# The delta scan split eleven to five: the larger part in PSUM on VectorE, the smaller on GpSimd, sums on TensorE

## The reference: what is computed

```python
Sk = jnp.einsum('bhde,bhe->bhd', Sm, k_t)
delta = v_t - Sk
Sm = Sm + beta_t[..., None] * jnp.einsum('bhd,bhe->bhde', delta, k_t)
o_t = jnp.einsum('bhde,bhe->bhd', Sm, q_t)
```

## Time and profile before

| what | value |
|---|---|
| median of 3 runs | 2863.08 us |
| span of the profiled execution | 2862.5 us |
| PE, DVE, ACT, POOL busy | 1846.5, 1859.1, 941.8, 992.1 us |
| stage 2, from 1169.70 to 1586.05 us | 416.3 us |
| in 1173.8 to 1586.0: PE, DVE, POOL busy | 247.3, 366.2, 248.4 us |

### The profile page before, as it was taken

How to read it: one execution, slowest core, us unless ns; L and a number is a source line. 1 busy time by engine, 2 the same in 40 slices (tenths; PEclk the granted TensorE clock), 3 DMA queues, 4 the chain that set the end, 5 groups by cost and what they waited for, 6 DMA issues and landing times. The chain is left out here.

```text
span 2862.5 us, 43966 instructions
## 1 busy us (share of the span) xinstructions
PE 1846.5 (65%) x9776; PEld 929.6 (32%) x9776; DVE 1859.1 (65%) x5482; ACT 941.8 (33%) x1955; POOL 992.1 (35%) x1512
## 2 busy tenths in 40 slices
PE   2499999998407913366566107447999999950493
PEld 1133333333305702233333004322333333350373
DVE  6488778784512237899999358558888888643123
ACT  2256656566102300000000003233656656720131
POOL 3022222223373410455665055301222222336442
PEclk8589999999558956676776558767999999965697
DMA  2501111110013450000000300130111111001344
GB/s 71 196 22 25 26 26 25 25 25 2 5 50 115 133 137 4 0 0 0 0 0 4 33 15 15 44 99 28 31 26 26 24 25 24 2 0 40 94 137 128
DMA packets 109051, 120.23 MB, mean 42 GB/s; under 512 B 31248, under 2 KB 71568, under 8 KB 107664
## 3 DMA queue, kind: packets, MB, share of 16 engines
q1 hardware_dynamic: 92304, 96.50, 13.1%
q0 software_dynamic: 8192, 16.86, 1.7%
q10 hardware_dynamic: 8320, 4.19, 0.6%
HBM read 71.01 MB, written 45.71 MB: 41 GB/s over the span
## 5 line engine op out<-in xcount | busy, mean ns | idle before, releaser
L719 DVE CUSTOM_DVE_ANT_0 pA<-pA,causal 128x512 f32<-128x512 f32 (+3 forms) x1536 | 823.6, 582 | 181.2 <-PE pA L562 168.5
L763 ACT ACTIVATE wt<-pB 128x512 f32<-128x512 f32 (+3 forms) x1536 | 653.9, 496 | 441.1 <-PE pB L603 435.4
L804 POOL TENSOR_SCALAR_AFFINE_SELECT wt<-wt 128x128 f32<-128x128 f32 x1024 | 290.6, 293 | 766.5 <-ACT wt L763 745.7
L562 PE MATMUL pA<-ka,qa 125*128 125x512 bf16 (+3 forms) x1536 | 487.2, 343 | 66.6 <-PEq L258 30.0
L603 PE MATMUL pB<-qa,ka 128*128 128x512 bf16 (+3 forms) x1536 | 450.5, 337 | 42.5 <-ACT wt L763 19.4
L1594 PE MATMUL g_pq<-g_proq,ident 128*128 128x256 f32 x512 | 247.3, 651 | 179.0 <-POOL g_proq L1547 179.0
L619 PE MATMUL pC<-wt,va 128*32 128x512 f32 (+3 forms) x3072 | 345.6, 497 | 0.3
L603 PEld LDWEIGHTS pB<-qa,ka 128*128 128x128 bf16 x1536 | 145.3, 97 | 418.8 <-ACT wt L763 256.0
L1594 PEld LDWEIGHTS g_pq<-g_proq,ident 128*128 128x128 f32 x512 | 138.5, 278 | 287.5 <-POOL g_proq L1547 207.2
L562 PEld LDWEIGHTS pA<-ka,qa 125*128 125x128 bf16 x1536 | 147.6, 98 | 249.5 <-DVE mx L719 163.6
L719 DVE DVE_READ_ACCUMULATOR2_ANT mx<- 128x1 f32 x1536 | 216.8, 141 | 0.0
(11 more groups left out here) (219 smaller groups left out, 2163.0 us busy)
## 6 DMA issues: line engine op xcount, KB each, us to landing
w<-in_L_ffn_fc_w_dram SPq DMA_DIRECT2D x64, 256.0 KB
qa<-qk_parts SPq DMA_DIRECT2D x192, 64.0 KB
ka<-qk_parts SPq DMA_DIRECT2D x192, 64.0 KB
xi<-xin SPq DMA_DIRECT2D x32, 258.0 KB
qk_parts<-qp SPq DMA_DIRECT2D x24, 256.0 KB, 2.4
qk_parts<-kp SPq DMA_DIRECT2D x24, 256.0 KB, 2.8
xin<-zero SPq DMA_DIRECT2D x4, 1032.0 KB, 7.1
y<-zero SPq DMA_DIRECT2D x4, 1024.0 KB, 12.6
```

The costliest lines, as they stand in the source:

```text
L562: pe.matmul(slot(s, n)[:, 0:b - a], qa[s.stage][0:MROW, h, i * P:(i + 1) * P], ka[s.stage][0:MROW, h, a:b], start=True, stop=True).then_in ...
L719: vec.tensor_tensor_reduce(out=slot(s, n)[:, 0:size], in0=slot(s, n)[:, 0:size], in1=mask, scale=1.0, scalar=LOWEST, op0=ALU.add, op1=ALU.max,
L763: act.activation(wt[g % NW][h][:, 0:e - a], pB[(g * GH + h) % NB][:, 0:e - a], ACT.Exp).then_inc(exp_done, 1)
L804: pool.affine_select(out=block_, in_=block_, compare_op=ALU.is_ge, fill=0.0, base=0, pattern=[[1, P]], channel_multiplier=-1).then_inc(mas ...
```

## The change

The heads are divided eleven to five in place of eight and eight, and each part stays with one engine. VectorE keeps eleven heads, with their matrix `Rv` in PSUM; GpSimd keeps five in `Rg` in SBUF. Each engine makes the key products, the outer products, the updates and the query products of its own heads. The sum over the last index and the subtraction of the values move to TensorE for both: eight matmuls against the identity and one against minus the identity, into `uv` (which VectorE reads in PSUM) and `pu` (which ScalarE copies to `ug` for GpSimd, which has no operand in PSUM here). The PSUM buffer of the query sums is doubled. TensorE's order for a token j is: deltas of VectorE's heads for j+1, deltas of GpSimd's heads for j+1, query sums of j. At the start the first matrix is made in SBUF and copied to PSUM by VectorE, and at the end it is copied back for the store, which is two DMAs now.

```diff
...
         FULL = [P, H, R2, HD]
...
+        HV = 11
+        HG = H - HV
+        PART_V, PART_G = [P, HV, R2, HD], [P, HG, R2, HD]
+        V_LINKS = 2
+        G_LINKS = 2
         with ExitStack() as in2:
             sb2 = lambda n, s, dt=F32: core.sb(in2, "g2_" + n, s, dt)
+            ps2 = lambda n, s, dt=F32: core.ps(in2, "g2_" + n, s, dt)
             sem2 = lambda n: core.sem(in2, "g2_" + n)
...
+            Rv, uv = ps2("Rv", PART_V), ps2("uv", [P, 512])
+            uv = uv[:, 0:HV * R2].rearrange("p (h r) -> p h r", r=R2)
+            Rg, ug = sb2("Rg", PART_G), sb2("ug", [P, HG, R2])
+            prod_v, prod_g = sb2("prod_v", PART_V), sb2("prod_g", PART_G)
             proq = [sb2(f"proq{i}", FULL) for i in range(2)]
...
+            minus = sb2("minus_ident", [P, P])
+            pu = ps2("pu", [P, HG, R2])
+            pq = [ps2(f"pq{i}", [P, H * R2]) for i in range(2)]
+            start, copied, chain_v, chain_g, kv_mult, uv_sum, kg_mult, ug_sum, ug_kept, qv_mult, qg_mult, q_sum, q_kept, end_kept, stored = (
+                sem2(n) for n in ("start", "copied", "chain_v", "chain_g", "kv_mult", "uv_sum", "kg_mult", "ug_sum", "ug_kept", "qv_mult",
+                                  "qg_mult", "q_sum", "q_kept", "end_kept", "stored"))
+
+            def heads(a, j, at, first, count):
+
+                begin = at + first * HD
+                return a[:, bass.ds(j, 1), begin:begin + count * HD].rearrange("p o (h r) -> p (o h) r", r=HD)
             def tokens(eng, one):
...
                 one(SEG - 2, 0)
                 one(SEG - 1, 1)
+            def more(j):
+                return not isinstance(j, int) or j < SEG - 1
+
+            def reused(j):
+                return not isinstance(j, int) or j >= 2
+
             with nc.Block() as block:
                 @block.gpsimd
                 def _(pool):
...
+                    pool.memset(prod_v[:, :, :, :], 0.0).then_inc(start, 1)
+                    pool.memset(Rg[:, :, :, :], 0.0).then_inc(start, 1)
+                    pool.memset(minus[:, :], 0.0).then_inc(start, 1)
+                    pool.wait_ge(start, 3)
+                    for whole, count in ((prod_v, HV), (Rg, HG)):
+                        eye = whole[:, :, HD:, :]
+                        pool.affine_select(out=eye, in_=eye, compare_op=ALU.not_equal, fill=1.0, base=0,
+                                           pattern=[[0, count], [1, HD], [-1, HD]], channel_multiplier=0).then_inc(start, 1)
+                    pool.affine_select(out=minus[:, :], in_=minus[:, :], compare_op=ALU.not_equal, fill=-1.0,
+                                       base=0, pattern=[[-1, P]], channel_multiplier=1).then_inc(start, 1)
                     def multiply(j):
...
+                        pool.tensor_tensor(prod_g[:, :, :, :], Rg[:, :, :, :],
+                                           heads(qkvb, j, D, HV, HG).unsqueeze(2).to_broadcast(PART_G),
+                                           ALU.mult).then_inc(kg_mult, 1)
                     def token(j, n):
...
+                        pool.wait_ge(ug_kept, j + 1)
+                        pool.tensor_tensor(prod_g[:, :, :, :], ug[:, :, :].unsqueeze(3).to_broadcast(PART_G),
+                                           heads(kbeta, j, 0, HV, HG).unsqueeze(2).to_broadcast(PART_G),
+                                           ALU.mult).then_inc(chain_g, 1)
+                        pool.wait_ge(chain_g, j * G_LINKS + 1)
+                        pool.tensor_tensor(Rg[:, :, :, :], Rg[:, :, :, :], prod_g[:, :, :, :],
+                                           ALU.subtract).then_inc(chain_g, 1)
+                        pool.wait_ge(chain_g, j * G_LINKS + 2)
+                        if more(j):
                             multiply(j + 1)
...
+                        if reused(j):
                             pool.wait_ge(q_sum, j - 1)
...
+                        pool.tensor_tensor(proq[n][:, HV:, :, :], Rg[:, :, :, :],
+                                           heads(qkvb, j, 0, HV, HG).unsqueeze(2).to_broadcast(PART_G),
+                                           ALU.mult).then_inc(qg_mult, 1)
+
+                    pool.wait_ge(start, 6)
                     multiply(0)
                     tokens(pool, token)
                 @block.vector
                 def _(vec):
...
+                    vec.wait_ge(start, 6)
+                    vec.tensor_copy(Rv[:, :, :, :], prod_v[:, :, :, :]).then_inc(copied, 1)
+                    vec.wait_ge(copied, 1)
                     def multiply(j):
...
+                        vec.tensor_tensor(prod_v[:, :, :, :], Rv[:, :, :, :],
+                                          heads(qkvb, j, D, 0, HV).unsqueeze(2).to_broadcast(PART_V),
+                                          ALU.mult).then_inc(kv_mult, 1)
+
+                    def query(j, n):
+                        if reused(j):
+                            vec.wait_ge(q_sum, j - 1)
+                        vec.tensor_tensor(proq[n][:, 0:HV, :, :], Rv[:, :, :, :],
+                                          heads(qkvb, j, 0, 0, HV).unsqueeze(2).to_broadcast(PART_V),
+                                          ALU.mult).then_inc(qv_mult, 1)
                     def token(j, n):
...
+                        vec.wait_ge(uv_sum, j + 1)
+                        vec.tensor_tensor(prod_v[:, :, :, :], uv.unsqueeze(3).to_broadcast(PART_V),
+                                          heads(kbeta, j, 0, 0, HV).unsqueeze(2).to_broadcast(PART_V),
+                                          ALU.mult).then_inc(chain_v, 1)
+                        vec.wait_ge(chain_v, j * V_LINKS + 1)
+                        vec.tensor_tensor(Rv[:, :, :, :], Rv[:, :, :, :], prod_v[:, :, :, :],
+                                          ALU.subtract).then_inc(chain_v, 1)
+                        vec.wait_ge(chain_v, j * V_LINKS + 2)
+                        if more(j):
                             multiply(j + 1)
+                        query(j, n)
                     multiply(0)
                     tokens(vec, token)
+                    vec.tensor_copy(prod_v[:, :, :, :], Rv[:, :, :, :]).then_inc(end_kept, 1)
                 @block.tensor
                 def _(pe):
+                    flat = lambda v: v.rearrange("p h r -> p (h r)")
+
+                    def vector_deltas(j):
+
+                        pe.wait_ge(kv_mult, j + 1)
+                        reached(pe, chain_v, j * V_LINKS)
+                        for e in range(HD):
+                            pe.matmul(flat(uv), c["ident"][:, :], flat(prod_v[:, :, :, e]), start=e == 0, stop=False)
+                        pe.matmul(uv[:, :, 0:HD], minus[:, :], heads(qkvb, j, 2 * D, 0, HV),
+                                  start=False, stop=True).then_inc(uv_sum, 1)
+
+                    def pool_deltas(j):
+
+                        pe.wait_ge(kg_mult, j + 1)
+                        reached(pe, ug_kept, j)
+                        for e in range(HD):
+                            pe.matmul(flat(pu[:, :, :]), c["ident"][:, :], flat(prod_g[:, :, :, e]),
+                                      start=e == 0, stop=False)
+                        pe.matmul(pu[:, :, 0:HD], minus[:, :], heads(qkvb, j, 2 * D, HV, HG),
+                                  start=False, stop=True).then_inc(ug_sum, 1)
+
                     def token(j, n):
...
+                        if more(j):
+                            vector_deltas(j + 1)
+                            pool_deltas(j + 1)
+                        pe.wait_ge(qv_mult, j + 1)
+                        pe.wait_ge(qg_mult, j + 1)
+                        if reused(j):
+                            pe.wait_ge(q_kept, j - 1)
                         for e in range(HD):
...
+                            last = pe.matmul(pq[n][:, :], c["ident"][:, :], flat(proq[n][:, :, :, e]),
                                              start=e == 0, stop=e == HD - 1)
                         last.then_inc(q_sum, 1)
+                    pe.wait_ge(start, 6)
+                    vector_deltas(0)
+                    pool_deltas(0)
                     tokens(pe, token)
                 @block.scalar
                 def _(act):
...
+                    def keep_delta(j):
+                        act.wait_ge(ug_sum, j + 1)
+                        act.copy(ug[:, :, :], pu[:, :, :]).then_inc(ug_kept, 1)
+
+                    def token(j, n):
+                        if more(j):
+                            keep_delta(j + 1)
                         act.wait_ge(q_sum, j + 1)
...
+                        act.copy(outs[:, bass.ds(j, 1), :, :].rearrange("p o h r -> p (o h r)"), pq[n][:, :]).then_inc(q_kept, 1)
+
+                    keep_delta(0)
+                    tokens(act, token)
                 @block.sync
                 def _(sp):
...
+                    sp.wait_ge(chain_g, SEG * G_LINKS)
+                    sp.dma_start(w["segments"][:, HV:, :].rearrange("p h x -> p (h x)"),
```

(31 more changed lines are left out.)

18 lines of the change are left out of this document (removed).

## The result

The changed kernel takes 2947.31 us, the median of 4 runs (2941.5 to 2950.78), beside 2865.79 us for the kernel before in 4 runs (the three above and one more): a ratio of 1.0286, 95% interval 1.0265 to 1.0307. It is 82 us slower; 2948 was forecast. The profiled execution has a span of 2939.8 us, 77.3 more than that of before.

A forecast was written before the change was run, and what follows sets the result against it. VectorE, with its waits for GpSimd, was taken to bound the scan at 12.56 us a token; TensorE at 15.3 us would replace it. The scan goes from 416.3 to 500.7 us, +84.4, giving 2948 us, range 2932 to 2990.

The forecast's parts named there:

- The main term: Scan: TensorE becomes the bound, 8192 strided column reads a token, 15.2 to 15.8 us, taken as 15.3.
- V: TensorE's group in the scan for the deltas of VectorE's heads: 5.3 us a token.
- P: TensorE's group in the scan for the deltas of GpSimd's heads: 2.5 us a token.
- Q: TensorE's query sums of the token before, in the scan: 7.4 us a token.
- the proportional end: TensorE's strided reads in the scan cost 1.80 ns a column and record: 14.75 us a token.
- the fixed part: Other end for TensorE's strided reads: 0.035 us a record plus 1.67 ns a column, 15.35 us a token.
- The clock: TensorE in the scan: busy throughout at clock 1.00, yet strided columns stay at 1.80 ns at either clock.
- The cover: Scan: P and Q, 9.9 us, cover VectorE's 5.0 us between V groups, even 9.8 with PSUM instructions twice as long.
- the rival in which a wait for VectorE takes TensorE's place: Scan: VectorE over 3.2 us an instruction in PSUM, loop above 15.3 us, time above 2948; 10% together with loads that show.
- The ends: Scan's start and finish: first V after 7.8 us, 18.1 until TensorE stops waiting, then to 500.7 us against 416.3 before.
- The rival that TensorE would stream at the contiguous price: Scan: strided matmuls at 0.84 ns a column, 7.6 us a token, 255 us, total 2702 us; chance 6%.
- Rival "loads stop hiding": TensorE in the scan: weight loads show behind narrow matmuls, 1.5 us a token, 48 us, 2996; 10% together with VectorE's wait.

The follow-up runs named there:

- e1: Changed kernel with matrices and all products stored last index first, so TensorE's operands are contiguous, plus a copy back at the end: 2731.59 us, ratio 0.9546.
- e3: Changed kernel with VectorE's key product made twice, once into a spare tile: 2950.4 us, ratio 1.0304 to the kernel before.
- e4: Changed kernel with the matrix of VectorE's eleven heads in SBUF in place of PSUM: 2951.01 us, ratio 1.0313 to the kernel before.
- e7: Changed kernel, query products only, with two of the eight last elements side by side (TensorE stride 8 bytes): 2833.58 us, ratio 0.9901.
- e2: Changed kernel with only the query products stored last index first, delta groups still at stride eight: 2822.66 us, ratio 0.9857.
- e5: Kernel of e1 with the matrix of VectorE's heads in SBUF in place of PSUM: 2777.68 us, ratio 0.9703 to the kernel before.

## Why the prediction was right, point by point

- The main term. 15.3 us of TensorE a token were forecast, 15.23 measured. Of its parts, V was put at 5.3 us and takes 5.30 (1401.96 to 1407.26), P at 2.5 and takes 2.51 (to 1409.77), Q at 7.4 and takes 7.42 (to 1417.19). The choice between the ends, proportional to columns or with a fixed part a record, is settled for the proportional end: 80 columns take 2.35 / 16 = 0.147 us a record (0.144 by proportion, 0.168 with the fixed part), 176 columns 5.10 / 16 = 0.319 (0.317 or 0.328). The 0.1 us that was added for waits between groups is not there: the groups join without a gap. The sum is closer than its terms: the strided columns take 14.87 us (14.75 forecast), the values 0.36 (0.45), the waits nothing (0.1).
- The clock. TensorE is at 1.00 from 1194 us on, as forecast, and the strided records didn't speed up. At the start of the scan it isn't: the first V begins at 0.50 and the second has a stretch of 0.50 in it, and they take 5.26 and 5.18 us from their start to the matmuls with the values, where V takes 5.10 at 1.00. In e1, with contiguous operands, the first takes 4.68 at 0.52 and a later one 2.48 at 0.99. So the price of the strided columns hardly depends on the clock here either.

```profile
1177.90:1180.00 2.10, 2.03 (x6) 0.50 0.00 0
```

- The cover. P and Q were said to cover VectorE's round of 5.0 us and even 9.8 us. e3 lengthened it by 1.6 us and e4 by 0.9, and the time stayed; no run made it as long as 9.8. VectorE's instructions were put at 1.60 us and take 1.61 to 1.63, far from the 3.2 us of the rival in which a wait for VectorE takes TensorE's place; GpSimd's at 1.45 and take 1.29 for the product with `kbeta` and 1.54 or 1.55 for the others, in sum 5.9 (5.8).
- The ends. The scan was put at 500.7 us and takes 499.15. The first V was to start 7.8 us after the first memset and does so 8.0 after (1177.97 - 1169.97); the wait for the second V, 5.0 less the 2.5 of P by the terms of the prediction, is 2.53. In the timeline of the start and the end:

```profile
1169.97 1.27 POOL L1539 MEMSET g_prod_v<- 128x1408 f32 x1 [152.83 <-POOLq L1351]
...
1177.97 5.44 PE L1623 MATMUL g_uv<-g_prod_v,ident 128*128 128x176 f32 x16 [18.70 <-DVE g_prod_v L1586]
...
1188.64 5.35 PE L1623 MATMUL g_uv<-g_prod_v,ident 128*128 128x176 f32 x16 [2.53 <-DVE g_prod_v L1586]
```

```profile
1669.12 0.32 SPq L1696 DMA_DIRECT2D g_Rt<-segments  x1
```

- The figure. That 2948 and 2947.31 are less than 1 us apart is luck: the scan came out 1.6 us shorter than forecast, the median of the kernel before is 2.7 us higher with its fourth run than with three, and the four runs of each of the two kernels spread over 9 and 10 us. What the runs bear out is the +84.4 us of the scan, where +82.8 was measured, and the terms that it is made of.
- The rival that TensorE would stream at the contiguous price is refuted for this kernel, and e1 makes it true by another layout. Its price was too low: 2702, while e1 takes 2731.59. P had been put at 1.3 us by its columns, where records of 80 contiguous columns stand 0.112 us apart, 1.94 us with the last record's end; and by the rival VectorE's round was to be last at 7.6 us, where TensorE is with 8.19. The 0.6 us a token are 19 of the 25 us by which the scan of e1 (280.47 us) is longer than the rival's 255.
- Rival "loads stop hiding": refuted, records of 80 strided columns stand 0.147 us apart although the weight load of each lasts 206 ns.

## What to carry to other kernels

Before work is moved to an idle engine, price it from that engine's rows of the same access pattern, not of the same operation: TensorE was idle 40% of the scan, and the pattern made its work of a token nearly twice as long. Where TensorE sums over an index against the identity, store that index outermost, or at least in pairs of neighbours (e7, 11.49 us a token where e2 with the index outermost has 11.32): with it outermost everywhere the same matmuls then took 8.19 us a token in place of 15.23, and the change is a gain of 4.5% instead of a loss of 2.9%. A fix of one engine's waiting (the matrix in PSUM) can be right and worth nothing until the engine that is last has room: nothing that the runs can tell in the kernel after, some 45 us in e1.

## What the runs showed of the hardware that was not expected

- Matmul records of the same width took nearly the same time at strides of 16 and 32 bytes (0.45 and 0.46 us for 256 columns) and nearly the contiguous time at 8 bytes (0.23, contiguous 0.22): a step, not a slope.
- VectorE's product of 1408 elements took 2637 ns when its output stepped 1024 bytes from element to element (e2), 1614 ns at 4 bytes; GpSimd's of 640 elements did not change (1555 ns, 1539 before). In e7, with two elements side by side, VectorE's took 1615 ns.
- VectorE's and GpSimd's instructions with SBUF operands took turns in e5: each ended 1.18 to 1.48 us after the end of the other engine's instruction inside which it had begun.
